# An attention block on one core: the place of one reciprocal and of U's loads

## What is computed

```python
h = group_norm(x, gn_w, gn_b)                     # 32 groups
hf = h.reshape(Bx, Cx, N)
qkv = jnp.einsum('oc,bcn->bon', qkv_w, hf) + qkv_b[None, :, None]
q, k, v = jnp.split(qkv, 3, axis=1)
q = q.transpose(0, 2, 1); v = v.transpose(0, 2, 1)
attn = jnp.einsum('bnc,bcm->bnm', q, k) * scale
attn = jax.nn.softmax(attn, axis=-1)
o = jnp.einsum('bnm,bmc->bnc', attn, v).transpose(0, 2, 1)
o = jnp.einsum('oc,bcn->bon', out_w, o) + out_b[None, :, None]
return x + o.reshape(Bx, Cx, Hx, Wx)
```

## Time and profile before

| | us |
|---|---|
| median of 3 runs | 1997.63 |
| lowest, highest | 1994.39, 1999.02 |
| the profiled execution | 1995.93 |
| its span, first to last instruction | 1994.1 |
| PE busy | 1977.3 (99%) |
| DVE busy | 1644.5 (82%) |
| ACT busy | 1121.0 (56%) |
| POOL busy | 448.8 (23%) |
| DMA, mean over the span | 79 GB/s |

### The profile page before, as it was taken

How to read it: one execution, slowest core, us unless ns; L and a number is a source line. 1 busy time by engine, 2 the same in 40 slices (tenths; PEclk the granted TensorE clock), 3 DMA queues, 4 the chain that set the end, 5 groups by cost and what they waited for, 6 DMA issues and landing times. The chain is left out here.

```text
span 1994.1 us, 26069 instructions
## 1 busy us (share of the span) xinstructions
PE 1977.3 (99%) x9895; PEld 1679.2 (84%) x9895; DVE 1644.5 (82%) x2010; ACT 1121.0 (56%) x1431; POOL 448.8 (23%) x306
## 2 busy tenths in 40 slices
PE   9999999999999999999999999999999999999999
PEld 7888888888888888888888888887888888878788
DVE  8896987969879698796978879697796987969866
ACT  6564645646465564645656467464565646556461
POOL 1122040231412213131230401314022131221311
PEclk9999999999999999999999999999999999999999
DMA  6305143060431504324042330614306043150411
GB/s 176 128 7 138 49 75 118 6 159 28 75 118 22 170 2 75 118 54 139 6 86 101 70 123 6 146 41 75 118 11 165 17 75 118 20 172 2 75 33 54
DMA packets 102637, 157.89 MB, mean 79 GB/s; under 512 B 49377, under 2 KB 51265, under 8 KB 102513
## 3 DMA queue, kind: packets, MB, share of 16 engines
q0 software_dynamic: 31264, 73.15, 17.5%
q1 hardware_dynamic: 71248, 83.08, 12.9%
HBM read 85.57 MB, written 68.26 MB: 77 GB/s over the span
## 5 line engine op out<-in xcount | busy, mean ns | idle before, releaser
L459 PE MATMUL ring<-r_hi 128*128 128x512 f32 (+1 forms) x1724 | 657.3, 381 | 0.6 <-ACT ring L932 0.4
L460 PE MATMUL ring<-r_lo,r_hi 128*128 128x512 f32 (+1 forms) x1724 | 656.4, 381 | 0.0
L461 PE MATMUL ring<-r_hi,r_lo 128*128 128x512 f32 (+1 forms) x1724 | 656.3, 381 | 0.0
L459 PEld LDWEIGHTS ring<-r_hi 128*128 128x128 f32 x1724 | 324.2, 188 | 64.1 <-DVE r_lo L1478 2.1
L461 PEld LDWEIGHTS ring<-r_hi,r_lo 128*128 128x128 f32 x1724 | 324.2, 188 | 62.0
L460 PEld LDWEIGHTS ring<-r_lo,r_hi 128*128 128x128 f32 x1724 | 324.3, 188 | 61.1
L881 ACT ACTIVATE stage<-ring,keybias 128x512 f32<-128x512 f32 x256 | 175.2, 685 | 164.2 <-PE ring L461 161.5
L1171 POOL PARTITION_ALL_REDUCE stage<-stage x32 | 127.2, 3976 | 460.3 <-DVE stage L1531 460.3
L854 ACT ACTIVATE stage<-ring,by_tile 128x512 f32<-128x512 f32 x120 | 82.5, 687 | 245.9 <-PE ring L461 245.9
L1463 DVE TENSOR_TENSOR r_lo<-stage,r_hi 128x1024 fp32r<-128x1024 f32 x128 | 182.1, 1452 | 0.0
L459 PE MATMUL ring<-h_hi,r_hi 128*128 128x512 f32 x444 | 172.8, 389 | 0.1
(11 more groups left out here) (199 smaller groups left out, 3903.0 us busy)
## 6 DMA issues: line engine op xcount, KB each, us to landing
xs<-x_in SPq DMA_DIRECT2D x64, 512.0 KB, 6.2
out<-xs SPq DMA_DIRECT2D x60, 512.0 KB, 5.4
out<-run_max POOLq DMA_DIRECT2D x60, 256.0 KB, 5.7
inv<-inv_row SPq DMA_DIRECT2D x32, 256.0 KB, 4.1
out<-spare POOLq DMA_DIRECT2D x30, 256.0 KB, 6.9
out<-all_max POOLq DMA_DIRECT2D x30, 256.0 KB, 5.1
r_hi<-g_dram POOLq DMA_DIRECT2D x15, 512.0 KB, 6.4
r_lo<-g_dram POOLq DMA_DIRECT2D x15, 512.0 KB, 6.5
```

The costliest lines, as they stand in the source:

```text
L459: nc.tensor.matmul(ps_out, st_hi, m_hi, start=first, stop=False, skip_group_check=goes_on)
L460: nc.tensor.matmul(ps_out, st_hi, m_lo, start=False, stop=False, skip_group_check=goes_on)
L461: return nc.tensor.matmul(ps_out, st_lo, m_hi, start=False, stop=last, skip_group_check=goes_on)
```

## The change

Two edits. On VectorE the reciprocal of half 1's sums, `inverse(b, 1)`, stands ahead of the four `scale_output(b, 0, c)` and no longer behind them. On POOL `load_u` waits for the end of the fourth score product (P_S2) ahead of all its four transfers; before, the two for A12 and S2 waited for the second (P_A12) and only the two for A11 for the fourth.

```diff
             def load_u(b):
-                pool.wait_ge(s_unit, unit(b, "S") + 4 * P_A12 + 4)
+                pool.wait_ge(s_unit, unit(b, "S") + 4 * P_S2 + 4)
                 count = 1 if b == 1 else 2
...
                     nc.gpsimd.dma_start(t[:, at:at + count, :], u_dram[side, :, 1:1 + count, :]).then_inc(s_uload, DMA)
-                pool.wait_ge(s_unit, unit(b, "S") + 4 * P_S2 + 4)
                 for side, t in ((0, r_hi), (1, r_lo)):
                     nc.gpsimd.dma_start(t[:, u_home(b, A11), :], u_dram[side, :, 0, :]).then_inc(s_uload, DMA)
...
                     h_combined(b + 1)
+                inverse(b, 1)
                 for c in range(CT):
                     scale_output(b, 0, c)
                     if not more:
                         whole_output(0, c)
-                inverse(b, 1)
```

## The result

The changed kernel takes **1983.78 us**, the median of 4 runs (1982.57 to 1984.37), against 1996.12 us for the kernel before on the same chip (1994.39 to 1999.02, 4 runs). The ratio is 0.993, with a 95% interval of 0.9913 to 0.9946: 12.3 us faster, where 16 were forecast. The profiled execution took 1984.35 us.

The account below looks back on a forecast made before the run. TensorE, busy nearly all the span, was taken as the bound, with 17.3 us of waiting. Winning 11.5 of 12 us T gaps and 4.5 of 5 us V gaps and starts gave 1995.9 - 16 = 1980 us, range 1976.5 to 1991.

Parts of the forecast that it names:

- The floor: TensorE's period per image: 120.82 us with no wait between; 17.3 us of the span is waiting, all that reordering can win.
- Part 2: POOL's U loads at the change of images: moving 1 MB later brings x 2.6 us earlier, a 2 us lead into V.
- The V gaps: TensorE's waits in the V stage, 0.8 us and less each; with starts of the outputs 5 us, 4.5 taken as won.
- either lead alone (2 us) exceeds the largest gap: Argument against half the gain: the reciprocal's move or U's move would each suffice to close TensorE's largest gap.
- Part 1: VectorE's reciprocal ahead of half 0's outputs: inv load issued 3.6 us earlier, remainders of h behind gain about 2 us.
- the price placed between 3.5 and 9.8 us: Time of half 1's inv load among the output accumulates, between these bounds; 6.1 us taken, landing at 1867.8.
- The reciprocal's wait: Rival: VectorE blocked until half 1's own sums land, 2010 us, chance 0.04; in the last image certain but free.
- So the remainders of h behind it gain about 2 us: VectorE behind half 1's outputs: the fourth output waits for all_max's accumulate, so remainders gain about 2 us, not 3.6.
- What is late next is TensorE itself: At the T stage, after the moved reciprocal: half 1's banks are complete only at the stage's end near 1868.
- the prediction's own signs of being wrong: Inv load over 9 us; long own-sums wait outside last image; wait in V's first product; gaps staying under a new name.
- No change: Rival: each gap closes but an equal one opens, say at the fourth scaled output awaiting all_max's accumulate; 1994 us, chance 0.07.
- half the gain: Rival: inverse load no faster among accumulates, or x hardly earlier; one part works, 6 to 10 us go; 1988 us, chance 0.19.

Follow-up runs that it names:

- The best version: Changed kernel with the second remainder of h moved ahead of half 1's scaled outputs, right behind the first: 1978.04 us, ratio 0.9903.

## Why the prediction was right, and where it was not

**The floor: right.** 120.82 us a period without a wait, and 17.3 us of waiting in all. The best version reaches it in 13 of 14 periods; 1.1 of the 17.3 us no order tried here won.

**Part 2, U's loads: right, and worth more than its share.** x came 2.7 us earlier in the stage shown (5.45 in place of 8.2 us behind its issue) and 2.3 us in the middle of the last 13 images, for 2.6 forecast. The lead that reached the first subtracted maximum, counted from the first issue for x, was 2.1 us in that stage (25.3 in place of 27.4 us) and 1.7 us in the middle, for 2 forecast. After, it is 25.3 us in 12 of these 13 images (25.2 in the other), where it was 25.7 to 29.0 before, so x no longer sets it. The V gaps closed (2.6 us to 0.3), U landed 7.4 to 9.9 us ahead of the V stage, and no transfer of U was waited for. The prediction had "either lead alone (2 us) exceeds the largest gap"; for part 2 that came near: 0.9931 alone, with four gaps at L1547 left of nine, the largest of 2.4 us.

**Part 1, up to half 1's outputs: right.** Store at 0.11 us behind half 0's start, 1.4 us to land, load 2.4 us behind the store. The load was the price placed between 3.5 and 9.8 us; all of them landed in 3.4 to 5.7 us:

```profile
DMA to landing us min/median/max: 3.4/4.5/5.7
```

I had taken 6.1; half 1's loads, the 15 that run among the accumulates, took 4.6 to 5.7 us. The fourth scaled output then waited for the accumulate of `all_max`, as said, by 1.4 us at most. The reciprocal's wait was free, in the last image too.

**Part 1, behind half 1's outputs: wrong.** The step that failed reads: "So the remainders of h behind it gain about 2 us", and with it "What is late next is TensorE itself". With the reciprocal alone the second remainder did start earlier against the T stage, by 2.1 us in the last one and 1.6 us in the middle of 15 images, but it ended only 0.4 us earlier in the last and 0.2 us later in the middle. The prediction left the remainder's own length at its usual 1.22 us, and it became 2.0 to 3.1, in the middle 3.09. In its place: the remainder, moved forward, met POOL's reduction and stood until that let it go. So "either lead alone" was false for part 1: alone it changed the time by nothing (1.0005), its 7.4 us of gaps having become 10.3 of another name, which is one of the prediction's own signs of being wrong. That is the rival "No change", right in form, and wrong as to who would be late: it named the accumulate. That wait is there too (8.5 us in 13 times, 1.2 at most), and is the part of the lead that the prediction did take off.

**What this cost the sum.** The forecast was 16 us; the spans give 11.5. The number came within the range although one of its two parts brought nothing: U's move alone gives 0.9931 and both parts 0.9933. That was luck as far as part 1 goes, since part 2's lead by itself closed most of the T gaps too. What is missing stands in few periods: 1.35 us in that with the other wait for L1289 (1378 us), and 3.9 us in that from 281.24 to 405.98, with 1.98 us of waiting for the remainder, and slower matmuls behind it. The windows are: stretch, length, busy time and count of PE, PEld, DVE, ACT and POOL, the granted clock, the DMA share and GB/s.

```profile
286.00:289.00 3.00, 1.02 (x5) 0.56 (x4) 3.00 (x2) 0.00 (x0) 3.00 (x1) 1.00 0.74 253
289.00:293.00 4.00, 4.00 (x12) 3.17 (x13) 2.04 (x2) 0.69 (x1) 2.88 (x4) 0.63 0.73 71
```

After a gap of 2 us the granted clock is 0.63 in the 4 us that follow, between its two levels of 2.4 and 1.2 GHz, and its matmuls stand 0.43 us apart in place of 0.23 for some 3 us. That is some 1.7 us more, nearly the gap again. The prediction had put "some more" for this. With the second remainder moved out of the way as well, both parts give 0.9903, a gain of 19 us, where the sum had 16 and rows 2 have 17.3 of waiting: for a kernel without that hold the sum was near, and too small if anything. Part of this is the second remainder's own (0.9975 alone).

**The range.** 1976.5 to 1991.0 had "half the gain" in it for other reasons (slow load, x no earlier) than the one that took 4 us.

## What to carry to other kernels

A step that is brought forward must be followed past the wait that it escapes: list what runs on the neighbouring engine at its new place, and which of the steps behind it share anything with that. Where the queues are full, first ask which of the early transfers nobody needs yet; moving 1 MB of them later was worth more here than shortening the chain that showed the longest waits. And when one gap is replaced by another of the same size, do the edits in pairs: the reciprocal, worth nothing alone or with U's move, was worth 3 to 9 us once the remainder was out of its way.

## What the hardware showed

**VectorE held by POOL.** A remainder (two inputs in SBUF, 1.22 us alone) that is under way while POOL's key-bias reduction (6.07 us) is, ends 5.56 to 5.57 us behind the reduction's start and not earlier; all 140 that were stretched beside a reduction of this length, in the 14 traces, end there. Started at +4.25 us a remainder took 1.31 us, at +4.34 us 1.22. The usual cost is up to 3.1 us, the most 5.61 us, of one that started 0.15 us behind the reduction (whose record is 6.25 us there). Of the four remainders of h beside the 4.03 us reduction of the own sums (from 1848.05) the second takes 3.26 us, in every such image and already in the kernel before: four in 6.67 us, where four subtractions of this size take 4.63 (L1457 in the changed kernel).

```profile
1847.77 6.67 DVE L1265 TENSOR_TENSOR h_lo<-stage,h_hi 128x1024 fp32r<-128x1024 f32 x4
```

The scaled outputs, with one input in PSUM, are not held: two of them ran beside the reduction that started at 1857.57 in the changed kernel, and of those into `all_max` none of 31 took over 0.694 us:

```profile
L1547 DVE TENSOR_TENSOR all_max<-ring,inv x31: 677/684/694, 148.2 to 1967.5; 128x512 f32<-128x512 f32 x31
```

Over all 14 traces 672 scaled outputs lie beside a reduction of POOL, and 0.694 us is the longest. The size of the tile is not what matters: L1412, a subtraction of 128x512 with both inputs in SBUF, took 5.21 us where it was held, and `r_lo<-ring,r_hi` of the same size with one input in PSUM 0.694 at most in the 41 times that it lay beside a reduction.

In the record such a hold shows as a longer VectorE instruction, with no idle time and no releaser, and is found only in the maximum of a group. The Trainium skill, SBUF — State Buffer (SBUF: two separate sides), has a pair of ports that VectorE and GpSimd share as an exclusive lock, asked for by a VectorE operation with two SBUF inputs against a GpSimd operation that reads SBUF, and kept by the first of them for its whole instruction. The traces agree as to who is held and who isn't. By "the whole instruction" the remainder would have had to start at +6.07 us and end at +7.3; measured it ended at +5.56, so here the release came about 4.3 us into the reduction (an estimate, from the end less the usual length; the starts at +4.25 and +4.34 above say the same). POOL's records are rough, but the end of this one is borne out: SP's store of the reduction's result, which waits for it, starts at +6.09 to +6.10 us. Why the release comes then, no run tells; other GpSimd operations were not tried.

**A gap of TensorE can cost twice, and need not.** The gap of 1.98 us above was followed by a stretch at a granted clock of 0.63. From 160 us on, the 14 traces have eight idle stretches of TensorE of 1.9 to 2.4 us, amid nearly full load. Five of them (1.97, 1.98, 2.04, 2.09, 2.38 us) were followed by seven to nine matmuls 0.43 us apart, at a mean granted clock of 0.57 to 0.66 in the 4 us behind the gap; three (1.91, 1.92, 2.12 us) were followed by a granted clock of 1.00 and 0.23 us from the second matmul on. Behind the shorter ones, of 1.60 us and less, no such stretch came: behind the gap of 1.05 us at 1378 us only the first matmul was long (0.50 us), and from the next but one on they stood 0.23 us apart again. What decides between the two, no run here tells.
